# Repair loop of an attention and expert kernel: the scores and the selection of one flagged tile are issued ahead of the transposes and the value product of the tile before it

## The chip, the cores and the metric

The kernel runs on one core of one Trainium2 chip. The time is device microseconds of one execution; the number compared is the median over several runs. A matrix engine (PE; its weight loads are shown apart as PEld), a vector engine (DVE), a scalar engine (ACT) and GpSimd (POOL) work side by side, each in its own program order. SyncE's queue (SPq) issues most DMAs, one after the other. The engines meet through semaphores.

## The reference

One transformer block on x (8 x 512 x 256) with a context of 8 x 1024 x 256: cross attention with 16 heads of width 16, in which every query keeps only its 32 highest scores, then a mixture of 8 experts. Only the attention matters here:

```python
scores = jnp.einsum('bhqd,bhkd->bhqk', q, k) / sqrt(DK)
scores = jnp.where(mask[:, None] == 0, NEG, scores)
vals, idx = jax.lax.top_k(scores, 32)
p = jax.nn.softmax(vals, axis=-1)
vg = jnp.take_along_axis(v[:, :, None, :, :], idx[..., None], axis=3)
ctx = jnp.einsum('bhqk,bhqkd->bhqd', p, vg)
```

## The kernel before

Six stages follow one another, each a block of its own with a barrier of all engines at its end: `project` (q, k and v into device memory), `attend`, `repair`, `route`, `experts`, `combine`.

`attend` works on 512 tiles, each of 128 queries of one head against all 1024 keys. It finds the 32nd highest score of each row from shortlists of 24 chunks, and counts how many scores lie below it. Where the count of a tile is not the expected one, or where the mask hides a key, the tile has to be done again. `repair` does that. It first turns counts into a list of flagged tile numbers (`flagged_tiles`) and their number (`total`), both read into registers by every engine. In these runs five tiles are flagged: each instruction of the loop body stands five times in the trace.

`flagged(eng, body)` is the loop of one engine: it reads the number, then for each `i` reads the tile's number and runs the body. For a tile, the bodies do this:

- SyncE (L747 to L764): waits for `free` (q, k and mask buffers may be overwritten), issues six DMAs of q, three of k, one of the mask (L751, L755, L758); then waits for `v_free` and issues the DMA of v (L761). Only then does it turn to the next tile.
- GpSimd: waits for `again`, fills the score tile `s` with -1e9, signals `cleared`.
- TensorE (L771 to L788): waits for q and k, multiplies the scores (L774, two matmuls of 512 columns, `scored`); waits for `probs`, turns the weights `ex` in eight transposes (L779); waits for the copy in SBUF and for v, multiplies the values (L784, eight f32 matmuls, which stand as x16 in the rows, `out_ready`); waits for `out_sb` and turns the product back (L788, `out_turned`).
- ScalarE: waits for `topped`, takes the exponential of all scores (L796); waits for `turned`, copies the transposes to SBUF (L799).
- VectorE (L843 to L867): waits for mask, `cleared` and `scored`; copies the unmasked scores into `s` (L848), and signals `free`; then four rounds of MAX8 (the next eight highest, L850 and L854) and MATCH_REPLACE8 (takes them out, L855); after the first MAX8 the negated maximum (L851, `topped`); then multiplies the exponentials by whether they were taken (L859), signals `again` and `probs`; waits for `out_ready`, copies the product (L862); waits for `out_turned`, inverts the denominator (L864) and writes 16 columns of `attn` (L865); at the very end it signals `v_free`.

`take(eng, signal)` is a wait that also clears the semaphore. `link(ins)` makes the engine wait for its own instruction. Every tile has one buffer of each kind, q, k, v, mask, `s`, `work`, `ex`, `exT` and the PSUM tiles.

Of the kernel before, what the change touches and what calls it, by code (L numbers as in the profile page):

```python
# [8 lines left out]
I32 = mybir.dt.int32  # L9
U32 = mybir.dt.uint32  # L10
ALU = mybir.AluOpType
# [638 lines left out]
def repair(nc, pl, io, scr, keep):  # L650

    G, TILES, KB, HG, DK, VW, KR, S2, QT = pl.G, pl.TILES, pl.KB, pl.HG, pl.DK, pl.VW, pl.KR, pl.S2, pl.QT
    NT = pl.ITER * TILES
    attn, lows, nonzero = keep["attn"], keep["lows"], keep["nonzero"]
    with ExitStack() as ctx:
        sb = lambda name, shape, dt=F32: ctx.enter_context(nc.sbuf_tensor(name, shape, dt))
# [9 lines left out]
        number = sb("g_number", [1, 1])  # L669
        eight = sb("g_eight", [1, 8])  # L670
        total = sb("g_total", [1, 1], I32)
        flagged_tiles = sb("g_flagged", [1, NT], I32)
        q = sb("g_q", [KR, P], BF16)
        k = sb("g_k", [KR, S2], BF16)
        v = sb("g_v", [P, KB, VW])
# [15 lines left out]
        own = sem("g_own")  # L691
# [3 lines left out]
        flags_ready = sem("g_flags_ready")  # L695
        free = sem("g_free")
        v_free = sem("g_v_free")
# [12 lines left out]
        out_turned = sem("g_out_turned")  # L710
        block = ctx.enter_context(nc.Block())

        def flagged(eng, body):

            eng.wait_ge(flags_ready, 1)
            n = eng.value_load(total[0:1, 0:1], min_val=0, max_val=NT)
            with eng.If(n > 0):
                with eng.Fori(0, n) as i:
                    tile = eng.value_load(flagged_tiles[0:1, bass.ds(i, 1)], min_val=0, max_val=NT - 1)
                    body(tile // TILES, tile % TILES // HG, tile % HG)  # L720

        def take(eng, signal, n=1):

            eng.wait_ge(signal, n)
            eng.sem_clear(signal)

        @block.gpsimd
        def _(pool):
            nc.gpsimd.memset(ident[:], 0.0).then_inc(made, 1)
            nc.gpsimd.memset(ones[:], 1.0).then_inc(made, 1)  # L730
            pool.wait_ge(made, 2)
            nc.gpsimd.affine_select(out=ident[:], in_=ident[:], compare_op=ALU.not_equal, fill=1.0, base=0,
                                    pattern=[[-1, P]], channel_multiplier=1).then_inc(made, 1)
            nc.gpsimd.iota(countdown[:], pattern=[[-1, NT]], base=NT, channel_multiplier=0,
                           allow_small_or_imprecise_dtypes=True).then_inc(made, 1)

            def tile(I, t, j):
                take(pool, again)
                nc.gpsimd.memset(s[:], NEG).then_inc(cleared, 1)

            flagged(pool, tile)
# [24 lines left out]
        @block.tensor  # L766
        def _(pe):
            pe.wait_ge(made, 3)
            nc.tensor.matmul(ps_t[1][0:1, 0:pl.TT], ones[:], nonzero[:], start=True, stop=True).then_inc(sums_ready, 1)

            def tile(I, t, j):  # L771
                take(pe, in_pe, 16 * (len(pl.q_spans) + len(pl.k_spans)))
                for h in range(S2 // 512):
                    mm = nc.tensor.matmul(ps_s[:, h * 512:(h + 1) * 512], q[:], k[:, h * 512:(h + 1) * 512],  # L774
                                          start=True, stop=True)
                mm.then_inc(scored, 1)
                take(pe, probs)
                for c in range(KB):
                    mm = nc.tensor.transpose(ps_t[c // 4][:, c % 4 * P:(c % 4 + 1) * P], ex[:, c * P:(c + 1) * P], ident[:])  # L779
                mm.then_inc(turned, 1)  # L780
                take(pe, turned_sb, 2)
                take(pe, in_v, 16)
                for c in range(KB):
                    mm = nc.tensor.matmul(ps_o[0:VW, :], v[:, c, :], exT[:, c * P:(c + 1) * P],  # L784
                                          start=(c == 0), stop=(c == KB - 1))
                mm.then_inc(out_ready, 1)
                take(pe, out_sb)
                nc.tensor.transpose(ps_u[:, 0:VW], outT[:], ident[0:VW, 0:VW]).then_inc(out_turned, 1)  # L788

            flagged(pe, tile)  # L790

        @block.scalar
        def _(act):
# [9 lines left out]
        @block.vector  # L803
        def _(dve):
            V = nc.vector
            count = [0]

            def link(ins):
                count[0] += 1
                ins.then_inc(own, 1)  # L810
                dve.wait_ge(own, count[0])


            dve.wait_ge(sums_ready, 1)
            link(V.tensor_scalar(mask_bad[:], ps_t[1][0:1, 0:pl.TT], float(P * S2), None, ALU.not_equal))
            dve.wait_ge(in_flat, 16)
            link(V.tensor_scalar(bad[:].rearrange("p (i n) -> p n i", n=TILES), flat[:], float(P * (S2 - pl.TOPK)), None,
                                 ALU.not_equal))
            by_mask = mask_bad[:].rearrange("p (b t) -> p b t", t=QT).unsqueeze(3).broadcast_to([1, pl.B, QT, HG])
            for g in range(G):  # L820
                part = bad[:].rearrange("p (b g t j) -> p b g t j", g=G, t=QT, j=HG)[:, :, g]
                ins = V.tensor_tensor(part, part, by_mask, ALU.max)
            link(ins)
            link(V.tensor_reduce(number[:], bad[:], AX_X, ALU.add))
            link(V.tensor_copy(total[:], number[:]))
            dve.wait_ge(made, 4)
            link(V.tensor_tensor(bad[:], bad[:], countdown[:], ALU.mult))

            n = dve.value_load(total[0:1, 0:1], min_val=0, max_val=NT)
            with dve.If(n > 0):  # L830
                with dve.Fori(0, (n + 7) // 8) as i:
                    dve.sem_clear(own)
                    count[0] = 0
                    link(V.max(eight[:], bad[:]))
                    link(V.match_replace(bad[:], eight[:], bad[:], -1.0))
                    link(V.tensor_scalar(flagged_tiles[:, bass.ds(i * 8, 8)], eight[:], -1.0, float(NT), ALU.mult, ALU.add))
            dve.sem_inc(free, 1)
            dve.sem_inc(v_free, 1)
            dve.sem_inc(again, 1)
            dve.sem_clear(own)  # L840
            dve.sem_inc(flags_ready, 1)

            def tile(I, t, j):  # L843
                count[0] = 0
                take(dve, in_dve, 16)
                take(dve, cleared)
                take(dve, scored)
                link(V.copy_predicated(s[:], mask[:], ps_s[:]))  # L848
                dve.sem_inc(free, 1)
                link(V.max(top[:, 0:8], s[:]))  # L850
                V.tensor_scalar(nmax[:], top[:, 0:1], -1.0, None, ALU.mult).then_inc(topped, 1)  # L851
                for r in range(pl.ROUNDS):
                    if r:
                        link(V.max(top[:, 8 * r:8 * r + 8], work[:]))  # L854
                    link(V.match_replace(work[:], top[:, 8 * r:8 * r + 8], work[:] if r else s[:], TAKEN))  # L855
                take(dve, expd)
                dve.sem_inc(again, 1)

                V.scalar_tensor_tensor(out=ex[:], in0=work[:], scalar=TAKEN / 2, in1=ex[:], op0=ALU.is_lt, op1=ALU.mult  # L859
                                       ).then_inc(probs, 1)  # L860
                take(dve, out_ready)
                V.tensor_copy(outT[:], ps_o[0:VW, :]).then_inc(out_sb, 1)  # L862
                take(dve, out_turned)
                link(V.reciprocal(rden[:], ps_u[:, DK:DK + 1]))  # L864
                link(V.tensor_scalar(attn[:, I * QT + t, bass.ds(j * DK, DK)], ps_u[:, 0:DK], rden[:], None, ALU.mult))  # L865
                dve.sem_clear(own)
                dve.sem_inc(v_free, 1)  # L867

            flagged(dve, tile)


def route(nc, pl, io, scr, keep):
# [749 lines left out]
```

## Time and profile before

| | |
|---|---|
| median of 3 runs | 3430.61 us (3429.76 to 3431.26) |
| the profiled execution, its own time | 3430.36 us |
| its span in the profile | 3428.6 us |
| repair: first DMA of a flagged tile to the last write of `attn` | 2265.61 to 2392.40 us |
| from the start of the first tile's masked copy (L848) to the last write of `attn` | 118.4 us |

Times in rows are microseconds from the start of the span. In a timeline row the columns are start, duration, engine, line, operation, tiles written and read, count, and in brackets how long the engine had been idle before it and what is taken to have ended that. Waits, register instructions and branches have no rows: they lie in the gaps. A wait for several semaphores is put down to the one that the profile sees last.

### The profile page before, as it was taken

What the parts mean: (1) busy time and instruction counts of PE and PEld (TensorE: products, weight loads), DVE (VectorE), ACT (ScalarE), POOL (GpSimd) and SP (SyncE); (2) the same over time, 40 slices, a digit from 0 to 9 for tenths busy, and PEclk for the clock granted to TensorE, in tenths of its full rate; (3) what the DMA queues carried; (4) which work ended last, traced back from release to release, by engine and by line L of the source; (5) the groups of instructions that cost most, each with busy time, mean ns of one, the idle gap of its engine ahead of it and who ended that gap; (6) DMA issues with size and microseconds to landing.
All of it is one profiled execution on the core that took longest, in us unless ns stands there. A gap on an engine that the chain in (4) does not pass through costs nothing. (4 is left out here: it accounts for less than half of the span.)

```text
span 3428.6 us, 77423 instructions
## 1 busy us (share of the span) xinstructions
PE 2727.2 (80%) x23469; PEld 1888.0 (55%) x23470; DVE 2805.7 (82%) x20098; ACT 1970.0 (57%) x3382; POOL 1826.1 (53%) x1278
## 2 busy tenths in 40 slices
PE   7838888888888888888888888832713999999990
PEld 5514445454544445454545454521603999999990
DVE  6749999999999999999999999944713766667653
ACT  2228888888888888888888888820200222222220
POOL 1017777777777777777777777710153111111107
PEclk9969999999999999999999999965856999999995
DMA  6961121121121111211211212011222112211206
GB/s 204 253 178 32 32 51 42 32 62 32 32 61 32 44 50 32 62 32 32 62 32 39 55 32 61 3 30 33 92 74 92 55 64 69 69 66 68 67 28 193
DMA packets 141983, 220.41 MB, mean 64 GB/s; under 512 B 22432, under 2 KB 103584, under 8 KB 138496
## 3 DMA queue, kind: packets, MB, share of 16 engines
q1 hardware_dynamic: 116608, 171.43, 18.3%
q0 software_dynamic: 9472, 29.37, 2.8%
q10 hardware_dynamic: 15488, 14.68, 1.3%
q8 instruction: 186, 3.05, 0.4%
q14 instruction: 229, 1.88, 0.2%
HBM read 142.02 MB, written 73.40 MB: 63 GB/s over the span
## 5 line engine op out<-in xcount | busy, mean ns | idle before, releaser
L568 DVE MAX8 a_cand<-a_sc 128x8 f32<-128x43 f32 (+1 forms) x12288 | 1682.8, 201 | 42.8 <-ACT a_sc L506 42.6
L640 POOL TENSOR_SCALAR a_low<-a_sc,a_top 128x1024 bf16<-128x1024 f32 x512 | 1456.2, 2844 | 0.0
L513 ACT ACTIVATE a_ex<-a_ps_e,a_nmax 128x1024 f32<-128x1024 f32 x512 | 577.7, 1128 | 149.4 <-PE a_ps_e L418 149.4
L506 ACT COPY a_sc<-a_ps_s 128x1024 f32<-128x1024 f32 x512 | 531.5, 1038 | 187.5 <-PE a_ps_s L406 170.7
L520 ACT COPY a_exT<-a_ps_t 128x512 f32<-128x512 f32 x1024 | 552.5, 602 | 0.3 <-PE a_ps_t L439 0.3
L439 PEld LDWEIGHTS a_ps_t<-a_ident,a_ex 128*128 128x128 f32 x4096 | 478.2, 140 | 102.1 <-ACT a_ex L513 1.0
L439 PE MATMUL a_ps_t<-a_ident,a_ex 128*128 128x128 f32 x4096 | 529.8, 272 | 0.8 <-ACT a_exT L520 0.8
L427 PE MATMUL a_ps_c<-a_low,a_row_of 128*16 128x512 bf16 x1024 | 307.2, 382 | 255.6 <-POOL a_low L640 214.7
L416 PE MATMUL a_ps_e<-a_ks,a_qs 96*128 96x512 bf16 x1024 | 394.3, 385 | 0.0
L418 PE MATMUL a_ps_e<-a_low,a_lowest 128*128 128x512 bf16 x1024 | 390.1, 381 | 0.0
L1292 POOL TENSOR_TENSOR e_wl<-e_raw,e_wh 128x2048 fp32r<-128x2048 f32 x24 | 110.5, 4603 | 519.9 <-DVE e_wh L1429 519.9
L1332 PE MATMUL e_ps_gu<-e_xh,e_wl 128*128 128x256 f32 x1280 | 363.9, 284 | 5.2 <-DVE e_xl L1412 4.0
L1333 PE MATMUL e_ps_gu<-e_xl,e_wh 128*128 128x256 f32 x1280 | 363.4, 284 | 0.0
L1334 PE MATMUL e_ps_gu<-e_xh,e_wh 128*128 128x256 f32 x1280 | 363.4, 284 | 0.0
L585 DVE MAX8 a_top<-a_work 128x8 f32<-128x80 f32 x1536 | 356.6, 232 | 0.1
L406 PE MATMUL a_ps_s<-a_ks,a_qs 96*128 96x512 bf16 x1024 | 309.7, 384 | 58.4 <-DMA a_vs<-scr_v 45.9
L639 POOL TENSOR_TENSOR a_nmax<-a_zeros,a_top 128x1 f32<-128x1 f32 x512 | 98.0, 191 | 477.9 <-DVE a_top L585 477.9
L427 PEld LDWEIGHTS a_ps_c<-a_low,a_row_of 128*16 128x16 bf16 x1024 | 49.5, 87 | 499.5 <-POOL a_low L640 390.2
L1392 ACT ACTIVATE e_th<-e_ps_gu 128x256 f32<-128x256 f32 x320 | 122.9, 384 | 338.4 <-PE e_ps_gu L1334 333.6
L1444 DVE SCALAR_TENSOR_TENSOR e_sg<-e_th,e_ps_gu 128x256 f32<-128x256 f32 x320 | 134.2, 420 | 195.8 <-ACT e_th L1392 185.0
L416 PEld LDWEIGHTS a_ps_e<-a_ks,a_qs 96*128 96x128 bf16 x1024 | 99.8, 97 | 282.9 <-issue 221.6
L449 PE MATMUL a_ps_ou<-a_exT,a_vs 128*32 128x128 f32 x8192 | 250.1, 274 | 1.5 <-ACT attn L495 1.5
(196 smaller groups left out, 4676.4 us busy)
## 6 DMA issues: line engine op xcount, KB each, us to landing
scr_v<-p_vp SPq DMA_DIRECT2D x32, 512.0 KB, 6.1
a_vs<-scr_v SPq DMA_DIRECT2D x32, 512.0 KB, 5.8
a_mask<-in_mask SPq DMA_DIRECT2D x32, 512.0 KB, 6.6
scr_k<-p_kp SPq DMA_DIRECT2D x96, 128.0 KB, 2.4
a_ks<-scr_k SPq DMA_DIRECT2D x32, 384.0 KB, 4.7
a_qs<-scr_q SPq DMA_DIRECT2D x192, 64.0 KB, 5.2
scr_disp<-a_zeros SPq DMA_DIRECT2D x32, 320.0 KB, 6.9
e_xin<-scr_disp SPq DMA_DIRECT2D x40, 256.0 KB, 2.7
```

The source lines that it names most:

```text
L416: nc.tensor.matmul(ps_e[:, half], qs[:, u, j, qt * P:(qt + 1) * P], ks[:, u, j, half], start=True, stop=False)
L418: mm = nc.tensor.matmul(ps_e[:, half], lowest[:], low[:, i % 2, half], start=False, stop=True)
L427: mm = nc.tensor.matmul(ps_c[0:TILES, :], row_of[:, i, :], low[:, i % 2, h * 512:(h + 1) * 512], start=(i == 0 and h == 0), stop=(i == TIL ...
L439: mm = nc.tensor.transpose(ps_t[h][:, c * P:(c + 1) * P], ex[:, i % 2, k * P:(k + 1) * P], ident[:])
L506: nc.scalar.copy(sc[:, i % 4, :], ps_s[:]).then_inc(copied[u], 1)
L513: nc.scalar.activation(ex[:, s % 2, :], ps_e[:], ACT.Exp, bias=nmax[:, v, s:s + 1]).then_inc(expd, 1)
L520: nc.scalar.copy(exT[:, t % 8, h * 512:(h + 1) * 512], ps_t[h][:]).then_inc(turned_sb, 1)
L568: ins = nc.vector.max(c[:, 8 + n:8 + n + 7 * CH + 1:CH], sc[:, i % 4, pl.cut[n]:pl.cut[n + 1]])
L640: nc.gpsimd.tensor_scalar(low[:, i % 2, :], sc[:, i % 4, :], top[:, u, i, pl.TOPK - 1:pl.TOPK], None, ALU.is_lt).then_inc(lowed, 1)
L1332: nc.tensor.matmul(out, al, bh, start=(k == 0), stop=False)
L1333: nc.tensor.matmul(out, ah, bl, start=False, stop=False)
L1334: mm = nc.tensor.matmul(out, ah, bh, start=False, stop=(k == n - 1))
```

## The change

The body of TensorE and that of VectorE are each cut in two and put together again one tile apart. TensorE: `scores` of the first tile; then in each turn of the loop `scores` of a tile and `values` (transposes, value product, turning back) of the tile ahead of it in the list; at the end `values` of the last one. VectorE: `select` of the first tile; then `select` of a tile, with two pieces of the tile ahead inside it: `take_out` (wait for `out_ready`, signal `v_free`, copy) after the fourth MAX8, and `normalise` (wait for `out_turned`, invert, write `attn`) after the last MATCH_REPLACE8; at the end `take_out` and `normalise` of the last one. The signal `v_free` moves from after the write of `attn` to before the copy. SyncE, GpSimd and ScalarE keep their bodies and their order. The list of flagged tiles is one entry longer and its entries begin at 1. TensorE and VectorE read two tile numbers in each turn.

```diff
@@ -669,7 +667,7 @@
         number = sb("g_number", [1, 1])
         eight = sb("g_eight", [1, 8])
         total = sb("g_total", [1, 1], I32)
-        flagged_tiles = sb("g_flagged", [1, NT], I32)
+        flagged_tiles = sb("g_flagged", [1, NT + 1], I32)
         q = sb("g_q", [KR, P], BF16)
         k = sb("g_k", [KR, S2], BF16)
         v = sb("g_v", [P, KB, VW])
@@ -710,14 +708,31 @@
         out_turned = sem("g_out_turned")
         block = ctx.enter_context(nc.Block())
 
+        def number_of(eng):
+            eng.wait_ge(flags_ready, 1)
+            return eng.value_load(total[0:1, 0:1], min_val=0, max_val=NT)
+
+        def tile_at(eng, i):
+
+            tile = eng.value_load(flagged_tiles[0:1, bass.ds(i, 1)], min_val=0, max_val=NT - 1)
+            return tile // TILES, tile % TILES // HG, tile % HG
+
         def flagged(eng, body):
 
-            eng.wait_ge(flags_ready, 1)
-            n = eng.value_load(total[0:1, 0:1], min_val=0, max_val=NT)
+            n = number_of(eng)
             with eng.If(n > 0):
                 with eng.Fori(0, n) as i:
-                    tile = eng.value_load(flagged_tiles[0:1, bass.ds(i, 1)], min_val=0, max_val=NT - 1)
-                    body(tile // TILES, tile % TILES // HG, tile % HG)
+                    body(*tile_at(eng, i + 1))
+
+        def flagged_in_turn(eng, first, then, last):
+
+            n = number_of(eng)
+            with eng.If(n > 0):
+                first(*tile_at(eng, 1))
+                with eng.If(n > 1):
+                    with eng.Fori(1, n) as i:
+                        then(tile_at(eng, i + 1), tile_at(eng, i))
+                last(*tile_at(eng, n))
 
         def take(eng, signal, n=1):
 
@@ -768,12 +783,14 @@
             pe.wait_ge(made, 3)
             nc.tensor.matmul(ps_t[1][0:1, 0:pl.TT], ones[:], nonzero[:], start=True, stop=True).then_inc(sums_ready, 1)
 
-            def tile(I, t, j):
+            def scores(I, t, j):
                 take(pe, in_pe, 16 * (len(pl.q_spans) + len(pl.k_spans)))
                 for h in range(S2 // 512):
                     mm = nc.tensor.matmul(ps_s[:, h * 512:(h + 1) * 512], q[:], k[:, h * 512:(h + 1) * 512],
                                           start=True, stop=True)
                 mm.then_inc(scored, 1)
+
+            def values(I, t, j):
                 take(pe, probs)
                 for c in range(KB):
                     mm = nc.tensor.transpose(ps_t[c // 4][:, c % 4 * P:(c % 4 + 1) * P], ex[:, c * P:(c + 1) * P], ident[:])
@@ -787,7 +804,11 @@
                 take(pe, out_sb)
                 nc.tensor.transpose(ps_u[:, 0:VW], outT[:], ident[0:VW, 0:VW]).then_inc(out_turned, 1)
 
-            flagged(pe, tile)
+            def step(tile, ahead):
+                scores(*tile)
+                values(*ahead)
+
+            flagged_in_turn(pe, scores, step, values)
 
         @block.scalar
         def _(act):
@@ -833,14 +854,14 @@
                     count[0] = 0
                     link(V.max(eight[:], bad[:]))
                     link(V.match_replace(bad[:], eight[:], bad[:], -1.0))
-                    link(V.tensor_scalar(flagged_tiles[:, bass.ds(i * 8, 8)], eight[:], -1.0, float(NT), ALU.mult, ALU.add))
+                    link(V.tensor_scalar(flagged_tiles[:, bass.ds(i * 8 + 1, 8)], eight[:], -1.0, float(NT), ALU.mult, ALU.add))
             dve.sem_inc(free, 1)
             dve.sem_inc(v_free, 1)
             dve.sem_inc(again, 1)
             dve.sem_clear(own)
             dve.sem_inc(flags_ready, 1)
 
-            def tile(I, t, j):
+            def select(I, t, j, ahead=None):
                 count[0] = 0
                 take(dve, in_dve, 16)
                 take(dve, cleared)
@@ -852,21 +873,37 @@
                 for r in range(pl.ROUNDS):
                     if r:
                         link(V.max(top[:, 8 * r:8 * r + 8], work[:]))
+                    if r == pl.ROUNDS - 1 and ahead is not None:
+                        take_out()
                     link(V.match_replace(work[:], top[:, 8 * r:8 * r + 8], work[:] if r else s[:], TAKEN))
+                if ahead is not None:
+                    normalise(*ahead)
                 take(dve, expd)
                 dve.sem_inc(again, 1)
 
                 V.scalar_tensor_tensor(out=ex[:], in0=work[:], scalar=TAKEN / 2, in1=ex[:], op0=ALU.is_lt, op1=ALU.mult
                                        ).then_inc(probs, 1)
+                dve.sem_clear(own)
+
+            def take_out():
                 take(dve, out_ready)
+                dve.sem_inc(v_free, 1)
                 V.tensor_copy(outT[:], ps_o[0:VW, :]).then_inc(out_sb, 1)
+
+            def normalise(I, t, j):
                 take(dve, out_turned)
                 link(V.reciprocal(rden[:], ps_u[:, DK:DK + 1]))
                 link(V.tensor_scalar(attn[:, I * QT + t, bass.ds(j * DK, DK)], ps_u[:, 0:DK], rden[:], None, ALU.mult))
-                dve.sem_clear(own)
-                dve.sem_inc(v_free, 1)
-
-            flagged(dve, tile)
+
+            def step(tile, ahead):
+                select(*tile, ahead)
+
+            def finish(I, t, j):
+                count[0] = 0
+                take_out()
+                normalise(I, t, j)
+
+            flagged_in_turn(dve, select, step, finish)
 
 
 def route(nc, pl, io, scr, keep):
```

## Rows read from the trace of the kernel before

**Rows 1.** The page: span, and busy time of each engine.

```profile
span 3428.6 us, 77423 instructions
...
PE 2727.2 (80%) x23469; PEld 1888.0 (55%) x23470; DVE 2805.7 (82%) x20098; ACT 1970.0 (57%) x3382; POOL 1826.1 (53%) x1278
```

**Rows 2.** Busy time of each engine in one tile's stretch (count), TensorE clock, DMA share.

```profile
core 0: us, PE busy (x) PEld busy (x) DVE busy (x) ACT busy (x) POOL busy (x), PEclk, DMA share, GB/s
...
2346.00:2370.00 24.00, 6.92 (x27) 4.54 (x27) 13.35 (x19) 2.22 (x3) 0.95 (x1) 0.50 0.15 37
```

**Rows 3.** Timeline of DVE, from the list of flags to the first tile.

```profile
2260.87 0.68 DVE L834 MAX8 g_eight<-g_bad 1x8 f32<-1x512 f32 x1 [1.66 <-remote]
...
2262.50 0.16 DVE L836 TENSOR_SCALAR g_flagged<-g_eight 1x8 f32 x1 [0.17 <-DVE g_bad L835]
```

**Rows 4.** Timeline of all engines, first tile, up to its masked copy.

```profile
2265.61 2.77 SPq L751 DMA_DIRECT2D g_q<-scr_q  x6
...
2270.18 0.35 SPq L758 DMA_DIRECT2D g_mask<-in_mask  x1
...
2271.55 1.03 PE L774 MATMUL g_ps_s<-g_k,g_q 96*128 96x512 bf16 x2 [16.31 <-DMA g_k<-scr_k]
2274.02 1.29 DVE L848 COPY_PREDICATED g_s<-g_mask,g_ps_s 128x1024 f32<-128x1024 int32 x1 [11.36 <-PE g_ps_s L774]
```

**Rows 5.** The tile g_mask: its DMAs, issue to landing, five tiles.

```profile
DMA to landing us min/median/max: 3.4/3.5/3.5
```

**Rows 6.** Timeline of all engines, fourth tile and the start of the fifth.

```profile
2344.94 0.57 SPq L761 DMA_DIRECT2D g_v<-scr_v  x1
2346.04 1.29 DVE L848 COPY_PREDICATED g_s<-g_mask,g_ps_s 128x1024 f32<-128x1024 int32 x1 [1.48 <-PE g_ps_s L774]
...
2348.00 2.73 SPq L751 DMA_DIRECT2D g_q<-scr_q  x6
...
2350.99 1.24 SPq L755 DMA_DIRECT2D g_k<-scr_k  x3
...
2352.54 0.35 SPq L758 DMA_DIRECT2D g_mask<-in_mask  x1
...
2355.28 1.23 DVE L854 MAX8 g_top<-g_work 128x8 f32<-128x1024 f32 x1
...
2356.62 1.21 DVE L855 MATCH_REPLACE8 g_work<-g_top,g_work 128x1024 f32<-128x1024 f32 x1
2358.01 1.23 DVE L859 SCALAR_TENSOR_TENSOR g_ex<-g_work,g_ex 128x1024 f32<-128x1024 f32 x1 [0.19 <-DVE g_work L855]
...
2359.39 1.97 PE L779 MATMUL g_ps_t<-g_ident,g_ex 128*128 128x128 f32 x8 [13.98 <-DVE g_ex L859]
2361.48 1.07 ACT L799 COPY g_exT<-g_ps_t 128x512 f32<-128x512 f32 x2 [11.33 <-PE g_ps_t L779]
...
2362.82 3.62 PE L784 MATMUL g_ps_o<-g_exT,g_v 128*32 128x128 f32 x16 [1.46 <-DMA g_v<-scr_v]
2366.57 0.28 DVE L862 COPY g_outT<-g_ps_o 32x128 f32<-32x128 f32 x1 [7.33 <-PE g_ps_o L784]
...
2367.01 0.31 PE L788 MATMUL g_ps_u<-g_ident,g_outT 32*128 32x32 f32 x1 [0.57 <-DVE g_outT L862]
2367.46 0.17 DVE L864 RECIPROCAL g_rden<-g_ps_u 128x1 f32<-128x1 f32 x1 [0.60 <-PE g_ps_u L788]
2368.24 0.23 DVE L865 TENSOR_SCALAR attn<-g_ps_u,g_rden 128x16 f32 x1 [0.61 <-DVE g_rden L864]
...
2368.31 1.03 PE L774 MATMUL g_ps_s<-g_k,g_q 96*128 96x512 bf16 x2 [0.99 <-DMA g_k<-scr_k]
2368.86 0.58 SPq L761 DMA_DIRECT2D g_v<-scr_v  x1
2369.97 1.29 DVE L848 COPY_PREDICATED g_s<-g_mask,g_ps_s 128x1024 f32<-128x1024 int32 x1 [1.49 <-PE g_ps_s L774]
```

**Rows 7.** Timeline of DVE, the last write of the stage.

```profile
2392.17 0.23 DVE L865 TENSOR_SCALAR attn<-g_ps_u,g_rden 128x16 f32 x1 [0.61 <-DVE g_rden L864]
```

## The prediction

> **What bounds the kernel now.** I read the page first. VectorE is busy for 82% of the span and TensorE for 80% [rows 1], so neither share says what a change in one stage is worth, and the stage has to be read by itself. The busy time by window comes second: in the 24.00 us of the fourth tile VectorE works 13.35 us, TensorE 6.92, ScalarE 2.22, GpSimd 0.95, and the DMA engines are busy for 0.15 [rows 2]. No engine is full. The stage is a chain in which they take turns; the order in time is the view that counts.
>
> In the timeline of the fourth tile [rows 6] the chain has two parts. VectorE's selection runs from the masked copy at 2346.04 to the end of L859 at 2359.24: 13.20 us with hardly a gap. Then the hand-overs: transposes 2359.39 to 2361.36, copies to 2362.55, value product 2362.82 to 2366.44, copy, turning back, inversion and the write of `attn` that ends at 2368.47. That is 9.23 us in which VectorE works 0.68. From there to the masked copy of the next tile at 2369.97 it takes 1.50 us. Period 23.93 us. The whole, from the first masked copy at 2274.02 [rows 4] to the last write at 2392.40 [rows 7], is 118.38 us, 3.5% of the span.
>
> What the reader should see beside it is SyncE's row of issues [rows 6]. The fourth tile's v is issued at 2344.94, just after the third tile is done. The fifth tile's q starts at 2348.00, 0.67 us after the masked copy has ended at 2347.33. Its k starts at 2350.99 and its mask at 2352.54. The mask takes 3.5 us to land [rows 5], so all is there at about 2356.0, 14 us before it is used. These loads are hidden today, and they cost a lot when they are not: at the first tile, where VectorE waits for them, the masked copy starts 8.41 us after the first q issue (2265.61 to 2274.02) [rows 4]. The profile puts that wait down to TensorE, but the scores ended at 2272.58. The mask landed at 2270.18 + 3.5 = 2273.68, 0.34 us before the copy. So the mask is what is late there, and TensorE is not.
>
> **The change, part by part.**
>
> Removed from the chain, for four of five tiles: the 9.23 us of hand-overs. They would lie beside the next tile's selection. TensorE's part fits: 1.97 + 3.62 + 0.31 and the copies are over 7.2 us after `scores` ends (2359.39 minus 0.15 to 2366.44, the same chain). The last tile keeps its 9.23 us.
>
> Added to VectorE inside a selection: `take_out` is a 0.28 us copy and two waits, say 0.4. `normalise` is 0.17 + 0.23 with the 0.61 gap between them and a small gap ahead, say 1.1 [rows 6]. TensorE's turning back (0.31, and about 0.15 on each side) lies under the last MATCH_REPLACE8 of 1.21 us; without that cover it would be 0.6 us. So a selection with a tile ahead takes 13.20 + 1.5 = 14.7 us. GpSimd's fill (0.95 [rows 2]) is signalled just ahead of L859, as before, and lies under its 1.23 us.
>
> Added at the turns: a second tile number read on TensorE and VectorE, a test for n > 1, a loop entry after the first tile, and an exit. No row shows these alone. Bounds for the way from L859 to the next masked copy: not less than today's turn, 1.50 us; not more than the longest entry seen, from the list written at 2262.66 to SyncE's first issue at 2265.61, 2.95 us [rows 3, 4]. VectorE itself stood 1.66 us ahead of L834, for a read, a test and a loop entry [rows 3]. I take 2.5 after the first tile and 2.0 in a turn. This gives 13.2 + 2.5 = 15.7 us for the first period. If VectorE alone set the later ones they would be 14.7 + 2.0 = 16.7 us.
>
> It does not, and this is the step on which the forecast rests. SyncE's order is not changed: q, k, mask of a tile, then the wait for `v_free`, then v, then the next tile. While a tile's v can't be issued, nothing of the following tile is. `v_free` for the tile ahead now comes in the middle of the next selection, after the fourth MAX8, at 2356.51 minus 2346.04 = 10.47 us after its masked copy [rows 6]. It can't come earlier, although the product is there some 5 us before that (below). What is queued behind that wait on SyncE is v, six q, three k and the mask, and TensorE and VectorE both wait for these. Counting from the masked copy of a tile:
> - 10.47: `take_out` signals `v_free`;
> - plus 0.39: v is issued, as from the end of the write of `attn`, where the signal stands today (2368.24 + 0.23 = 2368.47), to 2368.86 [rows 6];
> - plus 0.57: its issue;
> - plus the turn of SyncE's loop up to the first q. The trace bounds it: at least the 0.67 from signal to first q less the signal's travel, say 0.6; at most 2348.00 minus 2345.51 (the end of v's issue) = 2.49, since q then waited for the copy. The nearest row is TensorE's own turn, from 2367.32 to 2368.31, 0.99. I add the 0.67 for the addresses and take 1.65;
> - plus 8.41: from the first q to the masked copy of the next tile [rows 4].
>
> Sum 21.5 us (20.4 to 22.3) for each period after the first. The second tile's own loads are not held, since its `free` comes with the first masked copy and `v_free` was given at the start. But the third, fourth and fifth are. TensorE stands at its wait for k with `values` of the tile ahead behind it, from about 14.8 us after the masked copy (the end of L859 and 0.15), and the scores end at 20.0, so they are delayed by some 5 us. They are still over some 5.8 us into the next selection (the scores end 1.44 us before the copy at the first tile, and the chain is 7.2), 4.7 us ahead of `take_out`, so this adds nothing.
>
> After: 15.7 + 3 x 21.5 + 14.7 + 9.2 = 104.1 us, against 118.4. Gain 14.3 us. On the profiled execution's own 3430.36 us (span 3428.6 and 1.8 around it) this gives 3416.1; the median shown is 0.25 above that execution, so 3416.3. Without SyncE's order the sum would be 15.7 + 3 x 16.7 + 14.7 + 9.2 = 89.7, a gain of 28.7: half of what the overlap offers is lost.
>
> **The rivals.** *Full overlap*: VectorE sets the period, 16.7 us, gain 28.7, about 3402 us. For it: the DMA engines are nearly idle [rows 2], and the order is only a few issues. Against it: the chain above needs no bandwidth to be late, it is issue and landing. It would have to shrink from 11.0 us to 6.2.
>
> *Entries of new code cost more*. The same select code now stands twice, the value code too, and there are three jumps more. The longest entry today is 2.95 us, VectorE's row has 1.66 [rows 3, 4], and the turns of the loop at 1.50 show no stall. If the first entry and the last exit cost 2.3 us each beyond my figures (2.95 less SyncE's 0.67), and are in the open, the gain is 9.7, 3421. Beside it stands a rule of the Trainium skill, "Runtime: NRT & Kernel Launch", section on instruction fetch mechanics: a taken branch to code outside two 16 KB pages makes the sequencer fetch that page before it goes on. By the rule a far jump stalls; no row here shows one in the turns of this loop.
>
> *The wait inside the selection (slower)*. Today nothing stands behind the wait for `out_ready`. Now the last MATCH_REPLACE8 and L859 do, and TensorE reaches the value product only after the next scores. Should `out_ready` come late, every later piece waits. It decides from 4.7 us of lateness; to lose against before, it needs 14.3 / 3 more, 9.5 us of lateness in each of three tiles. That would be a value chain of 16.7 us where the row has 7.2. At 12 us late the time is 3416.3 + 3 x 7.3, 3438. Nothing in the trace lengthens it so.
>
> *SyncE's turn is dearer than its bound*, or the loads land later than at the first tile because v's transfer runs just ahead of q. No change that can be told needs a period of 24.0, 2.5 above mine.
>
> **How the numbers follow.** SyncE-bound: 0.72, own range 3412 to 3421 (periods of 20.4 to 22.3 make the gain 3.3 more or 2.4 less, the turns and exit about 2 either way). Dearer entries: 0.11. Full overlap: 0.09. Nearly no change: 0.05. Slower: 0.03. Range 3409 to 3424: the first two cases and a little beyond. A measurement of this kernel tells 0.2%, 6.9 us, from no change; only the last two cases lie within it or above it: faster 0.91, same 0.06, slower 0.03; since a stage so small is easily misjudged I give 0.88, 0.08, 0.04.
>
> **What would show it.** Masked copies about 15.7 us apart from first to second, then 21 to 22. SyncE's v issue in the middle of a selection, 0.4 us after the fourth MAX8, with q behind it, not 0.67 us after the masked copy. A gap of some 7 us on VectorE ahead of each masked copy from the third on, and the scores of the tile some 1.5 us ahead of that. `values` after `scores` and not right after L859. No wait at L862 but in the last tile. Wrong: gaps of 2 us ahead of the masked copies (full overlap), or a gap at L862 in the selection (the slower rival). The prediction fails most easily in the 1.65 us of SyncE's turn, which counts three times, and in the 2.5 us of the first entry.

## The result and the profile after

The changed kernel takes 3417.05 us (median of 6, 3415.15 to 3418.50), the kernel before 3430.94 us (median of 6) beside it. The ratio is 0.9957, 95% interval 0.9944 to 0.9970: faster by 0.43%, 13.9 us. The forecast was 3416.3 us, a gain of 14.3. A second set of five gave 3415.84 us, ratio 0.9958 (0.9944 to 0.9972).

The page of the changed kernel, span and busy time of each engine, beside [rows 1]:

```profile
span 3416.6 us, 77468 instructions
...
PE 2730.1 (80%) x23469; PEld 1891.0 (55%) x23470; DVE 2807.0 (82%) x20098; ACT 1970.2 (58%) x3382; POOL 1826.1 (53%) x1278
```

The shares say as little as before; VectorE is busy for 2807.0 us against 2805.7. The work is the same, its order in time is not. The timeline of all engines from the first flagged tile's masked copy to the product of the second; L869 is the masked copy, L871 and L875 MAX8, L884 the multiply, L891 the copy of the product, L895 and L896 the inversion and the write of `attn`, L789 the scores, L796 the transposes, L801 the value product, and L766, L770, L773, L776 the issues of q, k, mask and v. "remote" in brackets stands where the row names no instruction that ended the wait:

```profile
2277.62 1.29 DVE L869 COPY_PREDICATED g_s<-g_mask,g_ps_s 128x1024 f32<-128x1024 int32 x1 [11.49 <-PE g_ps_s L789]
...
2289.61 1.23 DVE L884 SCALAR_TENSOR_TENSOR g_ex<-g_work,g_ex 128x1024 f32<-128x1024 f32 x1 [0.19 <-DVE g_work L878]
...
2290.99 1.97 PE L796 MATMUL g_ps_t<-g_ident,g_ex 128*128 128x128 f32 x8 [4.48 <-DVE g_ex L884]
2291.66 1.35 DVE L869 COPY_PREDICATED g_s<-g_mask,g_ps_s 128x1024 f32<-128x1024 int32 x1 [0.82 <-remote]
...
2300.97 1.23 DVE L875 MAX8 g_top<-g_work 128x8 f32<-128x1024 f32 x1
2302.38 0.28 DVE L891 COPY g_outT<-g_ps_o 32x128 f32<-32x128 f32 x1 [0.18 <-remote]
2302.58 0.60 SPq L776 DMA_DIRECT2D g_v<-scr_v  x1
...
2304.79 2.73 SPq L766 DMA_DIRECT2D g_q<-scr_q  x6
...
2305.21 1.22 DVE L884 SCALAR_TENSOR_TENSOR g_ex<-g_work,g_ex 128x1024 f32<-128x1024 f32 x1 [0.18 <-remote]
...
2307.78 1.24 SPq L770 DMA_DIRECT2D g_k<-scr_k  x3
2309.32 0.35 SPq L773 DMA_DIRECT2D g_mask<-in_mask  x1
...
2310.63 1.03 PE L789 MATMUL g_ps_s<-g_k,g_q 96*128 96x512 bf16 x2 [7.51 <-DMA g_k<-scr_k]
...
2311.45 1.91 PE L796 MATMUL g_ps_t<-g_ident,g_ex 128*128 128x128 f32 x8
...
2313.11 1.31 DVE L869 COPY_PREDICATED g_s<-g_mask,g_ps_s 128x1024 f32<-128x1024 int32 x1 [6.68 <-PE g_ps_s L789]
...
2314.82 3.62 PE L801 MATMUL g_ps_o<-g_exT,g_v 128*32 128x128 f32 x16 [1.46 <-DMA g_v<-scr_v]
```

Read down the masked copies: 2277.62, 2291.66, 2313.11. The first period is 14.04 us, the second 21.45; the third and fourth, not shown, are 21.38 and 21.45. Before they were 24.14, 23.96, 23.92 and 23.93, the last of them in [rows 6]. In the second period of the changed kernel VectorE ends its selection at 2306.43 and then stands for 6.68 us. SyncE's rows show what it stands for. v goes out at 2302.58, in the middle of the selection, and q, k and mask of the next tile come behind it. Before, q went out 0.67 us after the masked copy and the mask was there long before its use [rows 5, 6]. The profile names TensorE as what ended the wait. But the scores end at 2311.66, and the masked copy starts 1.45 us later. The tile view of g_mask in this trace, issue to landing:

```profile
DMA to landing us min/median/max: 3.4/3.5/3.6
```

So the mask, issued at 2309.32, lands at about 2312.8, 0.3 us ahead of the masked copy. The transposes wait from 2306.43 to 2311.45 behind scores that wait for k.

The end of the stage, last tile:

```profile
2355.94 1.33 DVE L869 COPY_PREDICATED g_s<-g_mask,g_ps_s 128x1024 f32<-128x1024 int32 x1 [6.70 <-PE g_ps_s L789]
...
2366.66 0.28 DVE L891 COPY g_outT<-g_ps_o 32x128 f32<-32x128 f32 x1 [0.19 <-remote]
...
2369.49 1.23 DVE L884 SCALAR_TENSOR_TENSOR g_ex<-g_work,g_ex 128x1024 f32<-128x1024 f32 x1 [0.19 <-remote]
...
2377.72 0.28 DVE L891 COPY g_outT<-g_ps_o 32x128 f32<-32x128 f32 x1 [7.01 <-PE g_ps_o L801]
...
2379.32 0.23 DVE L896 TENSOR_SCALAR attn<-g_ps_u,g_rden 128x16 f32 x1 [0.61 <-DVE g_rden L895]
```

From the last masked copy to the end of the last write it is 23.61 us, and the stage from first masked copy to last write 101.93 us, against 118.38 [rows 4, 7].

### The profile page after: what moved, and what is told of

Same layout as the page of the kernel before. It is cut to its first block and busy times, and to the rows that moved or that the text cites. A ratio compares the mean times of both kernels' runs of the same rounds, so it can differ in the third digit from the quotient of the medians.

```text
span 3416.6 us, 77468 instructions
## 1 busy us (share of the span) xinstructions
PE 2730.1 (80%) x23469; PEld 1891.0 (55%) x23470; DVE 2807.0 (82%) x20098; ACT 1970.2 (58%) x3382; POOL 1826.1 (53%) x1278
```

## The experiments

"Stage" is always from the start of the first masked copy to the end of the last write of `attn`. Periods are from one masked copy to the next.

| kernel | periods, us | stage, us | one profiled execution, us |
|---|---|---|---|
| before | 24.14, 23.96, 23.92, 23.93 | 118.38 | 3430.36 |
| before, again | 24.14, 23.94, 23.88, 23.90 | 118.27 | 3436.30 |
| before, v_free early | 24.15, 23.95, 23.93, 23.92 | 118.44 | 3432.37 |
| before, list of tiles shifted | 24.05, 23.96, 23.93, 23.91 | 118.29 | 3431.53 |
| changed | 14.04, 21.45, 21.38, 21.45 | 101.93 | 3418.29 |
| changed, again | 14.03, 21.56, 21.55, 21.43 | 102.61 | 3412.15 |
| changed, v_free late | 14.04, 24.23, 24.17, 24.16 | 110.66 | 3424.75 |
| changed, take_out a round earlier | 14.03, 18.88, 18.80, 18.86 | 94.61 | 3412.11 |
| changed, mask first | 14.03, 20.83, 20.81, 20.78 | 100.15 | 3418.41 |
| changed, SyncE one tile apart too | 14.04, 15.76, 15.70, 15.69 | 85.23 | 3398.09 |
| the same, take_out a round earlier | 14.03, 15.75, 15.71, 15.68 | 85.22 | 3401.63 |
| the same, turn in the open | 15.33, 17.04, 17.00, 17.00 | 90.40 | 3407.19 |
| changed, v from ScalarE | 14.03, 15.77, 15.71, 15.70 | 84.91 | 3398.17 |

Each row is one profiled execution; a median of several runs is given where there is one. Repeated, the stage came back within 0.7 us (changed kernel) and 0.1 us (kernel before). The whole execution did not, which is taken up below.

**SyncE's order.** The theory was that SyncE's queue behind `v_free` sets the period; the rivals were TensorE's order and the landing of the loads. SyncE's body is cut as the other two are:

```diff
-            def tile(I, t, j):
+            def loads(I, t, j):
                 take(sp, free)
...
+            def load_v(I, t, j):
                 take(sp, v_free)
                 sp.dma_start(v[:], ...
-            flagged(sp, tile)
+            def step(tile, ahead):
+                loads(*tile)
+                load_v(*ahead)
+
+            flagged_in_turn(sp, loads, step, load_v)
```

> The changed kernel, with SyncE also one tile apart: q, k and mask of a tile are issued first, and only then does it wait for v_free and issue v of the tile ahead. Theory S (SyncE's order behind v_free sets the period of 21.4 us): the wait for v_free no longer holds q, k and mask, VectorE sets the period, 14.8 us of selection plus the 0.8 us turn seen after the first tile, 15.6 us; the stage from the first masked copy to the last write goes from 101.9 to about 84.5 us, the whole to 3399.6 us. Rival T (TensorE's order, scores ahead of the value product, sets it): the period stays near 21 us, since that order is unchanged. Rival L (landing of the loads): the period stays above 18 us, and VectorE still waits for the mask.

Timeline of all engines, third tile to the start of the fourth. The issue of v is L778 here, and the lines behind SyncE's body are six higher (scores L795, masked copy L875, multiply L890, copy of the product L897):

```profile
2304.79 1.32 DVE L875 COPY_PREDICATED g_s<-g_mask,g_ps_s 128x1024 f32<-128x1024 int32 x1 [0.99 <-PE g_ps_s L795]
...
2306.79 2.73 SPq L766 DMA_DIRECT2D g_q<-scr_q  x6
...
2309.78 1.24 SPq L770 DMA_DIRECT2D g_k<-scr_k  x3
...
2311.33 0.35 SPq L773 DMA_DIRECT2D g_mask<-in_mask  x1
...
2315.48 0.28 DVE L897 COPY g_outT<-g_ps_o 32x128 f32<-32x128 f32 x1 [0.19 <-remote]
...
2315.78 0.58 SPq L778 DMA_DIRECT2D g_v<-scr_v  x1
...
2317.99 1.03 PE L795 MATMUL g_ps_s<-g_k,g_q 96*128 96x512 bf16 x2 [1.76 <-DMA g_k<-scr_k]
2318.31 1.23 DVE L890 SCALAR_TENSOR_TENSOR g_ex<-g_work,g_ex 128x1024 f32<-128x1024 f32 x1 [0.19 <-remote]
...
2320.49 1.32 DVE L875 COPY_PREDICATED g_s<-g_mask,g_ps_s 128x1024 f32<-128x1024 int32 x1 [0.95 <-PE g_ps_s L795]
```

q starts 2.0 us after the masked copy again, the mask is out at 2311.33, and v follows by itself at 2315.78. The scores are done at 2319.02, before the multiply ends. VectorE works from copy to copy. Period 15.7 us, time 3397.24 us (median of 4), ratio 0.9900 (0.9882 to 0.9918). The theory had 15.6 and 84.5 us; the rivals' 21 and 18 are out. Against the changed kernel it is a further 20 us on the medians, which are of two sets of runs, and 16.7 in the stage.

**How much the place of the signal counts.** If the queue is a chain that hangs on `v_free`, a signal one round earlier must shorten each period by one round. `take_out` stands ahead of the third MATCH_REPLACE8:

```diff
-                    if r == pl.ROUNDS - 1 and ahead is not None:
+                    if r == pl.ROUNDS - 2 and ahead is not None:
                         take_out()
```

> The changed kernel, with take_out (and v_free in it) after the third MAX8 instead of the fourth. Theory S: the signal comes one round, 2.59 us, earlier, and each period from the third masked copy on shrinks by just that, 21.4 to 18.8 us; stage 101.9 to 94.2 us. The product is there 5.3 us after the masked copy, ahead of the third MAX8's end at 7.9, so no new wait at the copy of the product. Rival T or L: the period moves by less than 1 us.

Timeline, third tile to the fourth:

```profile
2311.30 1.30 DVE L869 COPY_PREDICATED g_s<-g_mask,g_ps_s 128x1024 f32<-128x1024 int32 x1 [4.11 <-PE g_ps_s L789]
...
2319.38 0.28 DVE L891 COPY g_outT<-g_ps_o 32x128 f32<-32x128 f32 x1 [0.19 <-remote]
2319.58 0.58 SPq L776 DMA_DIRECT2D g_v<-scr_v  x1
...
2321.78 2.73 SPq L766 DMA_DIRECT2D g_q<-scr_q  x6
...
2330.10 1.33 DVE L869 COPY_PREDICATED g_s<-g_mask,g_ps_s 128x1024 f32<-128x1024 int32 x1 [4.08 <-PE g_ps_s L789]
```

v goes out 8.28 us after the masked copy (changed kernel: 10.9), q 2.20 us after v, the next masked copy 8.32 us after q. The period is 18.80 to 18.88 us, 2.6 less. The copy of the product is not late: 0.19 us of idle time before it. `take_out` has moved as a whole, the copy with its signal, and the chain behind the signal has kept its lengths. Which of the two counts, the copy or the signal, the next experiments tell.

The same edit on the version with SyncE's order cut:

> The version with SyncE's order one tile apart, with take_out one round earlier as well. On the changed kernel the same edit was worth 2.6 us a period. Theory S: with SyncE off the path it is worth nothing, periods 15.7 us within 0.1, stage 85.2 us. Rival (an earlier copy of the product helps by itself, through TensorE that waits for it): the period falls by more than 0.3 us.

Periods 15.75, 15.71, 15.68, stage 85.22: worth nothing where the queue isn't on the path, though v goes out 8.4 us after the masked copy here and 11.0 without the edit. So an earlier copy of the product and an earlier v gain nothing by themselves.

**The moved signal alone.** On the kernel before:

```diff
                 take(dve, out_ready)
+                dve.sem_inc(v_free, 1)
                 V.tensor_copy(outT[:], ps_o[0:VW, :]).then_inc(out_sb, 1)
...
                 dve.sem_clear(own)
-                dve.sem_inc(v_free, 1)
```

> The kernel before, with v_free alone moved to where the changed kernel has it, ahead of the copy of the product. Theory S: nothing waits behind v there, as q, k and mask of the next tile land some 14 us before use; v is issued about 1.8 us earlier, the period stays 23.93 us within 0.1. Rival (the moved signal itself brings part of the gain): the period falls by 1 us or more.

Periods and stage are those of before, though v goes out 20.8 us after the masked copy instead of 22.8 (third tile). And the changed kernel with the signal back behind the write:

```diff
                 take(dve, out_ready)
-                dve.sem_inc(v_free, 1)
                 V.tensor_copy(outT[:], ps_o[0:VW, :]).then_inc(out_sb, 1)
...
                 link(V.tensor_scalar(attn[:, I * QT + t, bass.ds(j * DK, DK)], ...
+                dve.sem_inc(v_free, 1)
```

> The changed kernel, with one part undone: v_free is signalled after the write of attn, as in the kernel before, and not ahead of the copy of the product. Theory S: v goes out 0.39 us after that write, 13.7 us after the masked copy instead of 10.9, so each period from the third masked copy on grows by 2.8 to 24.2 us, longer than the 23.93 of the kernel before; only the first period (14.0 us) keeps a gain, and the stage is 110.4 us, the whole some 3425 us. Rival T or L: the period moves by less than 1 us.

Timeline, third tile to the fourth (the write of `attn` is L895 here):

```profile
2314.97 1.33 DVE L869 COPY_PREDICATED g_s<-g_mask,g_ps_s 128x1024 f32<-128x1024 int32 x1 [9.37 <-PE g_ps_s L789]
...
2328.04 0.23 DVE L895 TENSOR_SCALAR attn<-g_ps_u,g_rden 128x16 f32 x1 [0.63 <-DVE g_rden L894]
...
2328.62 0.58 SPq L776 DMA_DIRECT2D g_v<-scr_v  x1
...
2330.82 2.73 SPq L766 DMA_DIRECT2D g_q<-scr_q  x6
...
2339.14 1.32 DVE L869 COPY_PREDICATED g_s<-g_mask,g_ps_s 128x1024 f32<-128x1024 int32 x1 [9.33 <-PE g_ps_s L789]
```

v waits for the write that ends at 2328.27, and the period is 24.2 us, longer than without any overlap. All that is left of the gain is in the first period, whose loads don't hang on the signal. So a line that does nothing on the kernel before is worth 8.1 to 8.7 us of stage on the changed one.

**Which load is late.** The profile says that TensorE releases the masked copy, the prediction that the mask does.

```diff
             def tile(I, t, j):
                 take(sp, free)
+                sp.dma_start(mask[:], ...).then_inc(in_dve, 16)
                 for term, part, n in pl.q_spans:
...
-                sp.dma_start(mask[:], ...).then_inc(in_dve, 16)
                 take(sp, v_free)
```

> The changed kernel, with the mask issued ahead of q and k instead of behind them. My reading that the mask lands last, 0.3 us ahead of the masked copy, while the scores ended 1.4 us ahead of it: now k is last, the masked copy follows the end of the scores by 0.15 to 0.5 us, and the period falls from 21.4 to about 20.7 us (q and k are 0.5 us later, the 1.3 us behind the scores is gone). Rival, the reading of the profile that TensorE releases the masked copy: it keeps its 1.4 us behind the scores, and the period grows by 0.5 us to 21.9.

Timeline, ahead of the fourth tile's masked copy:

```profile
2326.67 0.38 SPq L765 DMA_DIRECT2D g_mask<-in_mask  x1
...
2327.40 2.73 SPq L768 DMA_DIRECT2D g_q<-scr_q  x6
2330.39 1.24 SPq L772 DMA_DIRECT2D g_k<-scr_k  x3
...
2333.27 1.03 PE L789 MATMUL g_ps_s<-g_k,g_q 96*128 96x512 bf16 x2 [8.19 <-DMA g_k<-scr_k]
...
2334.45 1.32 DVE L869 COPY_PREDICATED g_s<-g_mask,g_ps_s 128x1024 f32<-128x1024 int32 x1 [6.05 <-PE g_ps_s L789]
```

The scores end at 2334.30, the masked copy starts 0.15 us later. The period is 20.8 us, 0.6 less, as expected. The rival's 21.9 is out. The row of the masked copy still names TensorE, and here it is right.

**Whose queue.** The edit takes v off SyncE and keeps all else, the release at 10.5 us too:

```diff
                 nc.scalar.activation(ex[:], s[:], ACT.Exp, bias=nmax[:]).then_inc(expd, 1)
+                take(act, v_free)
+                act.dma_start(v[:], ...).then_inc(in_v, 16)
                 take(act, turned)
```

> The changed kernel, with SyncE's body left in its order but v, and the wait for v_free ahead of it, taken out of it and issued from ScalarE, behind the exponential and ahead of its wait for the transposes. ScalarE has nothing to do between 3 and 17 us after a masked copy. Theory S (what costs is that q, k and mask stand in one queue behind v_free, not v itself or when it is released): the periods are those of the version with SyncE's order one tile apart, 15.7 us, stage 85.2 us, 3397 us. Rival (the release at 10.5 us is what holds, in whatever queue): periods stay at 21 us.

Timeline of the third tile, with ScalarE's queue as ACTq (L786 the scores, L793 the transposes, L814 the exponential, L816 the issue of v):

```profile
2304.86 1.33 DVE L869 COPY_PREDICATED g_s<-g_mask,g_ps_s 128x1024 f32<-128x1024 int32 x1 [0.99 <-PE g_ps_s L786]
2306.11 1.07 ACT L820 COPY g_exT<-g_ps_t 128x512 f32<-128x512 f32 x2 [12.83 <-PE g_ps_t L793]
...
2307.87 1.15 ACT L814 ACTIVATE g_ex<-g_s,g_nmax 128x1024 f32<-128x1024 f32 x1 [0.69 <-DVE g_nmax L872]
...
2315.91 0.58 ACTq L816 DMA_DIRECT2D g_v<-scr_v  x1
...
2320.57 1.33 DVE L869 COPY_PREDICATED g_s<-g_mask,g_ps_s 128x1024 f32<-128x1024 int32 x1 [0.95 <-PE g_ps_s L786]
```

Periods 15.70 to 15.77, 3398.20 us (median of 4), ratio 0.9902 (0.9886 to 0.9919). v goes out 11.05 us after the masked copy, as late as it did (10.9), from an engine that has had nothing to do since its exponential ended at 2309.02, and costs nothing there.

**The turn.** The first period was forecast with 2.5 us from the multiply to the next masked copy and had 0.82. One tiny linked instruction behind the multiply, on the version with SyncE's order cut:

```diff
                 V.scalar_tensor_tensor(out=ex[:], ...).then_inc(probs, 1)
+                link(V.tensor_scalar(nmax[:], top[:, 0:1], -1.0, None, ALU.mult))
                 dve.sem_clear(own)
```

> The version with SyncE's order one tile apart, where VectorE sets the period (15.7 us), with one more tiny instruction (0.15 us, it writes the negated maximum again) behind L884, for which VectorE waits. My reading of the cheap turn: VectorE's sequencer goes through the loop's branch, the two reads of tile numbers and the waits while L884 still runs, so only 0.8 to 1.0 of some 2.1 us show; behind a wait for its own instruction, as in the kernel before, all of it shows. Then the way from the end of the multiply to the masked copy grows from 0.95 to 1.8 us or more, and the period to 16.5 to 16.9 us. Rival (a turn costs 0.8 us, wherever it lies): the period grows by the instruction alone, to 15.9 us.

Timeline of VectorE (L890 the multiply, L892 the added instruction, L875 the masked copy):

```profile
2324.70 1.22 DVE L890 SCALAR_TENSOR_TENSOR g_ex<-g_work,g_ex 128x1024 f32<-128x1024 f32 x1 [0.19 <-remote]
2325.85 0.15 DVE L892 TENSOR_SCALAR g_nmax<-g_top 128x1 f32<-128x1 f32 x1
2328.18 1.32 DVE L875 COPY_PREDICATED g_s<-g_mask,g_ps_s 128x1024 f32<-128x1024 int32 x1 [2.19 <-remote]
```

From the end of the multiply to the masked copy it is now 2.26 us, where it was 0.95, and the period 17.0 instead of 15.7, a little over what was expected. The turn costs about 2.2 us from the added instruction's end, and some 1.2 of them lay under the multiply. The rival's 15.9 is out. After the first tile, where the forecast had its 2.5 us, the same way is 2.13 us here. The branch and the reads themselves have no rows, so that it is these which run under the multiply is argued from this difference.

**Where the rest of the size went.** The stage gained more than the whole did.

> The changed kernel once more, for the size. In its profile the stage was 16.5 us shorter than before, 101.9 against 118.4, but the whole execution only about 12 us, since the stages ahead of the repair ended 3.5 us later than in the profile of before and those behind it took 1 us more. If that is chance from execution to execution, the stage repeats within 0.3 us at 101.9 and the start of the attention lies anywhere between 226 and 231 us; if the changed program itself is slower ahead of the repair, it lies above 230 us again. Time 3417 us, within 1.5.

> The kernel before, with only the list of flagged tiles one entry longer and its entries from 1 on. The stage stays at 118.4 us within 0.3. For the stages ahead of it this is a second program that differs from before only there: the start of the attention, 226.5 and 226.4 us in the two programs that are almost the kernel before and 228.2 to 230.5 in four that carry the change, tells chance (a value of 228 or more here) from an effect of the changed program (226.5 again).

> The kernel before, once more. The stage repeats at 118.4 us within 0.3. The start of the attention was 226.4 to 227.0 us in three programs without the change, and 225.9 to 231.8 in seven with it. If that is chance, this one may lie anywhere from 226 to 232; if programs without the change start earlier, it lies below 227.5 again.

The stage came back at 102.61 us, 0.7 more than the first time where 0.3 was expected; 0.4 of that is one faster value product in the first profile (last section). What lies ahead of it did not. The row of the attention's first loads, by the tile view of its q buffer (count, shortest, median and longest in ns, first and last start), of the changed kernel's repeat and then of the repeat of the kernel before:

```profile
L381 SPq DMA_DIRECT2D a_qs<-scr_q x192: 311/420/939, 225.9 to 2135.7; - x192
```

```profile
L381 SPq DMA_DIRECT2D a_qs<-scr_q x192: 310/420/901, 231.4 to 2140.6; - x192
```

The first issue of the attention's loads lay at 225.9 us this time (230.5 in the first profile), and in the last repeat of the kernel before at 231.4 (226.5 in the first). The shifted list had 227.0, which decided nothing by itself. The programs with the change lie between 225.9 and 232.3 us, those without it between 226.4 and 231.4: the start of the attention varies from execution to execution by itself, change or not. What follows the last write of `attn` varies too, from 1034.3 to 1038.7 us over the thirteen profiles. The start alone moves the time by up to 6 us, enough to account for what lies between the medians' 13.9 and the stage's 15.8 to 16.5 us. All runs of the changed kernel together, and all of the kernel before, give medians of 3416.8 us (11 runs) and 3431.8 us (28 runs, one of 7014.73 us left out), a gain of 15 us.

## Why the prediction was right

*What was removed.* The hand-overs of four tiles no longer stand behind a selection. That held: L891 waits 7.01 us in the last tile only, and 0.18 or 0.19 us in the others.

*What was added to a selection.* 14.7 us forecast, 14.75 to 14.78 measured (2291.66 to 2306.43), the last MATCH_REPLACE8 covering the turning back as expected.

*The step on which it rested.* SyncE's queue behind `v_free`: period 21.5 forecast, 21.4 measured. By its terms, from the second masked copy to the third: to v's issue 10.9 us (2291.66 to 2302.58; forecast 10.86), v's issue 0.60 (0.57), to the first q 1.61 (1.65), from there to the masked copy 8.32 (8.41). The term that seemed least certain, SyncE's turn, was bounded between 0.6 and 2.49 and came within 0.04 of the forecast. That closeness is partly luck: the 1.65 was put together from TensorE's own turn (0.99) and SyncE's 0.67 from signal to first q, and no run shows these two as its parts. The signal's place (2.6 us for one round), its undoing (24.2), the order (15.7) and the queue (15.7) show that it is this chain and not TensorE or the transfers as such.

*TensorE's delay.* Forecast some 5 us later transposes, without effect. They were 5.0 us late (2306.43 to 2311.45), and the value product ended 5.3 us into the next selection (2318.44 against 2313.11), 5 us ahead of its use. The slower rival, a wait for the product inside the selection, did not come about: L891 waits no longer than 0.19 us there.

*The mis-sized terms.* The first turn: 2.5 forecast, 0.82 measured, 1.7 us too much. The bounds had been 1.50 to 2.95, and the value lies below both, because the lower one was taken from the old kernel's turn as a floor. That turn stands behind a wait for VectorE's own write, the new one behind an instruction that it doesn't wait for. Where it was made to wait, the way was 2.13 us, within the bounds. In the later turns, with SyncE's order cut, it was 0.92 to 1.00 us, where the forecast had 2.0. The last tile took 23.6 and 24.0 us in the two profiles of the changed kernel, as forecast (14.7 + 9.2). The entries of new code showed no cost beside this: the first multiply ends 13.22 us after its copy as before, and the next masked copy starts 0.82 us later. At the exit the last transposes start 0.15 us after the last multiply (2370.72 to 2370.87), as before, and VectorE's own exit lies inside its wait of 7.01 us. So that rival is out here. A stall of the kind that the Trainium skill names ("Runtime: NRT & Kernel Launch", instruction fetch mechanics) shows in none of these rows. Whether any of the jumps leaves the two pages of that rule, and what such a jump would cost, no run here shows.

*Full overlap.* Forecast at 16.7 us a period and 3402 us if SyncE's order did not bind; with that order cut it is 15.7 and 3397, each turn being 1 us cheaper than assumed and the first entry 1.7 us.

So the stage gained 15.8 to 16.5 us where 14.3 were forecast, and most of the difference, 1.7 us, is that first turn. That the median still came within 0.8 us of the forecast is partly luck: the executions differ by 6 us ahead of the stage, and here that hid the mis-sized term.

## What to carry to other kernels

When two stages of a loop are put one tile apart, look at every queue that serves both: it may have to be put apart as well. List for each queue what it waits for and what stands behind that wait. Here one wait in a queue that was idle most of the time cost half of the overlap; putting its loads one tile apart too, or moving one DMA to an engine with nothing to do, won it back. The place of a release counted one for one here where the loads on the path were queued behind it, and not at all where they were not. For the cost of a loop's turn, ask whether the engine waits for its last instruction: if it doesn't, part of the turn lies under that instruction.

## What the runs showed that was not expected

- A turn of VectorE's loop with two numbers read from memory takes 2.2 us in the open and shows only 0.9 to 1.0 us behind an instruction of 1.23 us for which VectorE does not wait; the first entry has 2.1 and 0.8.
- The start of the attention, with nothing changed ahead of it, lay between 225.9 and 232.3 us in thirteen profiled executions. A stage's own time, repeated within 0.7 us, judges a change of this size better than the whole.
- In the changed kernel's first profile TensorE's last value product took 3.24 us (2374.29 to 2377.53) at a mean granted clock of 0.58 (between the levels of 1.2 and 2.4 GHz) instead of 3.62 at 0.50, the lower level. Two other profiles have 3.34 and 3.32 us at 0.56 there (mask first, v from ScalarE). Ahead of it TensorE had done its eight transposes at 0.50 (2370.87 to 2372.84) and stood for 1.46 us, but it did the same in the executions where the product took 3.62, so what raised the clock stays open. It accounts for 0.4 of the 0.7 us between the stage's 101.93 and 102.61.
